# Decays of a selective scan in four buffers, the fourth in SBUF, each made one scan earlier

## What is computed

```
h  = layernorm(x) * (1 + scale) + shift;  h = h[:, idx]
xm, z = split(h @ W_in);  xm = silu(causal_conv(xm) + conv_b)
dtr, B, C = split(xm @ W_xp)                    # 64, 16, 16 wide
dt = softplus(dtr @ W_dt + b_dt)                # 1024 channels
for t:  hst = hst * exp(dt_t * A) + (dt_t * x_t) * B_t      # 1024 channels x 16 states
        y_t = sum_s hst * C_t
y = (y + xm * D) * silu(z);  out = x + gate * (y @ W_out)[:, idx]
```

## Time and profile before

| | before |
|---|---|
| median of 3 runs | 3013.91 us (3012.91 to 3016.35) |
| the profiled execution's own time | 3009.61 us |
| its span in the profile | 3007.8 us |
| DVE busy, share of the span | 2466.3 us, 82% |
| PE busy | 2648.0 us, 88% |
| POOL busy | 1883.4 us, 63% |
| ACT busy | 1621.8 us, 54% |
| TensorE clock granted, mean | 0.949 |

### The profile page before, as it was taken

How to read it: one execution, slowest core, us unless ns; L and a number is a source line. 1 busy time by engine, 2 the same in 40 slices (tenths; PEclk the granted TensorE clock), 3 DMA queues, 4 the chain that set the end, 5 groups by cost and what they waited for, 6 DMA issues and landing times. The chain is left out here.

```text
span 3007.8 us, 31819 instructions
## 1 busy us (share of the span) xinstructions
PE 2648.0 (88%) x10790; PEld 1499.2 (50%) x10790; DVE 2466.3 (82%) x3111; ACT 1621.8 (54%) x2444; POOL 1883.4 (63%) x822
## 2 busy tenths in 40 slices
PE   7999999999999877988988988988888897897974
PEld 3555555555555354554554554455455455454542
DVE  3566556666656599999999999999999998999993
ACT  1221322331332576776875875776676687586550
POOL 0131121222122396897998899799799799889991
PEclk9999999999999878999989999999999998998976
DMA  6102231231233444555664575665575566566653
GB/s 216 36 28 85 69 106 42 91 112 36 91 112 116 135 98 97 118 126 119 151 148 122 143 164 115 146 158 120 133 161 130 133 148 147 126 142 137 171 122 75
DMA packets 261604, 355.39 MB, mean 118 GB/s; under 512 B 21597, under 2 KB 115937, under 8 KB 261434
## 3 DMA queue, kind: packets, MB, share of 16 engines
q1 hardware_dynamic: 202024, 246.38, 26.8%
q0 software_dynamic: 55680, 105.93, 20.1%
q10 hardware_dynamic: 3730, 0.96, 0.2%
HBM read 215.56 MB, written 71.58 MB: 95 GB/s over the span
## 5 line engine op out<-in xcount | busy, mean ns | idle before, releaser
L2073 POOL TENSOR_TENSOR hs<-slots,b_wide 128x2048 f32<-128x2048 f32 x255 | 1270.5, 5011 | 142.8 <-PE bank L1589 142.6
L2267 DVE TENSOR_TENSOR_SCAN hs<-bank,hs 128x512 f32<-128x512 f32 x1024 | 1224.5, 1215 | 30.3 <-ACT bank L1846 25.3
L1846 ACT ACTIVATE bank<-dt,decay 128x512 f32<-128x512 f32 x1022 | 698.6, 691 | 540.7 <-DVE hs L2267 538.5
L1589 PE MATMUL bank<-ident,hs 128*128 128x128 f32 x4096 | 676.1, 295 | 240.1 <-DVE acc L2285 181.0
L1589 PEld LDWEIGHTS bank<-ident,hs 128*128 128x128 f32 x4096 | 515.1, 150 | 724.3 <-issue 264.0
L2285 DVE SCALAR_TENSOR_TENSOR acc<-bank,c_t,acc 128x512 f32<-128x512 f32 x772 | 566.4, 734 | 43.0 <-PE bank L1589 40.2
L1541 PE MATMUL bank<-h_t,w_in 128*128 128x512 f32 x1024 | 510.8, 608 | 1.4 <-ACT h_t L1764 1.2
L2121 POOL DMA_DIRECT2D acc<-scaled x252 | 291.2, 1155 | 49.2 <-DMA acc<-scaled 35.0
L982 POOL TENSOR_TENSOR y_rs<-y_var,mhalf 128x8 f32<-128x8 f32 x8 | 15.8, 1972 | 393.5 <-DVE y_var L355 393.5
L1641 PE MATMUL bank<-w_y,values 128*128 128x512 f32 x512 | 253.0, 600 | 1.3 <-DVE values L2389 1.3
L800 PE MATMUL bank<-z_t,w_k 128*128 128x512 f32 x512 | 223.0, 594 | 4.3 <-DVE k_t L1009 3.2
(11 more groups left out here) (180 smaller groups left out, 3344.3 us busy)
## 6 DMA issues: line engine op xcount, KB each, us to landing
b_wide<-b_rows SPq DMA_DIRECT2D x256, 256.0 KB, 3.6
acc<-scaled POOLq DMA_DIRECT2D x252, 256.0 KB, 5.3
w_in<-in_L_cond_W_in SPq DMA_DIRECT2D x128, 256.0 KB, 4.4
res<-in_x SPq DMA_DIRECT2D x8, 2048.0 KB, 10.0
h_tiles<-h_t SPq DMA_DIRECT2D x56, 256.0 KB, 2.8
h_in<-h_tiles SPq DMA_DIRECT2D x56, 256.0 KB, 4.1
x_rows<-w_part POOLq DMA_DIRECT2D x28, 512.0 KB, 6.8
x_rows<-res SPq DMA_DIRECT2D x6, 2048.0 KB, 7.3
```

The source lines that it names most:

```text
L1589: last = nc.tensor.transpose(bank[:, j * P:(j + 1) * P], hs[:, slot, j, t * P:(t + 1) * P], ident[:, :])
L1846: nc.scalar.activation(decay_banks[N % 3][:, :], dt[:, H % 2, j, :], ACT.Exp, scale=g.decay[:, 4 * (H % 2) + j, s:s + 1]).then_inc(da_read ...
L2073: nc.gpsimd.tensor_tensor(hs[:, U % RING, :, :], slots[:, H % SLOTS, :, :], b_wide[:, U % B_RING, :].unsqueeze(1).to_broadcast([P, 4, CHUNK]),
L2267: nc.vector.tensor_tensor_scan(block, decay_banks[N % 3][:, :], block, 0.0, ALU.mult, ALU.add).then_inc(scanned, 1)
```

## The change

Four edits. First, a fourth decay buffer, `decay_tile`, is added in SBUF, and the decays go round four buffers instead of three. ACT makes decay N+4 in the step in which it made decay N+3, behind the same scan. The scans with N % 4 == 3, the fourth of each unit, 256 in all, now read their decay from SBUF; their other input, `hs`, always lay there. Second, the sum of the step sizes' second half on POOL moves from unit 7 to unit 9. Third, the first projection of a batch waits for each modulated group just ahead of the matmul that reads it, not for the last three groups ahead of the first matmul. Fourth, a small tile of row statistics, `raw`, is laid over 24 columns of `cols` that layer 0 no longer needs, which makes room for the new buffer.

```diff
+DECAY_RING = 4
-ADD_DT_AT = (28, 7)
+ADD_DT_AT = (28, 9)
-        g.raw = sb("raw1", [P, CT, 6])
+        g.raw = g.cols[:, 0:6 * CT].rearrange("p (t s) -> p t s", t=CT)
...
-        state_banks, decay_banks, work_banks = banks[0:2], banks[3:6], [banks[6], banks[7], banks[2]]
+        decay_tile = sb("decay_tile", [P, CHUNK])
+        state_banks, decay_banks, work_banks = banks[0:2], [*banks[3:6], decay_tile], [banks[6], banks[7], banks[2]]
...
-                    if stage == "xm" and m == 0:
-                        for i in range(KD)[-place.ring:]:
-                            need(pe, *read_by(place, "h", i))
-                for k in ks:
+                for k in ks:
+                    if stage == "xm" and m == 0:
+                        need(pe, *read_by(place, "h", k))
                     last = nc.tensor.matmul(...)
...
-                need(act, scanned, N - 2)
-                nc.scalar.activation(decay_banks[N % 3][:, :], dt[:, H % 2, j, :], ACT.Exp,
+                need(act, scanned, N - (DECAY_RING - 1))
+                nc.scalar.activation(decay_banks[N % DECAY_RING][:, :], dt[:, H % 2, j, :], ACT.Exp,
...
-                    if N + 3 < BLOCKS * BATCH:
-                        decays(N + 3)
+                    if N + DECAY_RING < BLOCKS * BATCH:
+                        decays(N + DECAY_RING)
...
+                decays(3)
                 for b in range(BATCH):
                     turn(b)
...
-                nc.vector.tensor_tensor_scan(block, decay_banks[N % 3][:, :], block, 0.0, ALU.mult, ALU.add)
+                nc.vector.tensor_tensor_scan(block, decay_banks[N % DECAY_RING][:, :], block, 0.0, ALU.mult, ALU.add)
```

More of the change, by code:

```diff
@@ L2266, in scan @@
                 block = hs[:, N // 4 % RING, N % 4, :]
-                nc.vector.tensor_tensor_scan(block, decay_banks[N % 3][:, :], block, 0.0, ALU.mult, ALU.add).then_inc(scanned, 1)
+                nc.vector.tensor_tensor_scan(block, decay_banks[N % DECAY_RING][:, :], block, 0.0, ALU.mult, ALU.add).then_inc(scanned, 1)
             def scan_on(it, b, c, q):
```

## The result

The changed kernel takes 3391.7 us (3389.08 to 3397.18, 4 runs) against 3013.41 us of the kernel before in the same session. The ratio is 1.126, 95% interval 1.124 to 1.128: 378 us slower. The direction and the mechanism were those forecast. The size was not: the loss is more than twice the forecast one, and the time lies above the range.

A forecast was written before the change was run, and what follows sets the result against it. The prediction took DVE, busy 96% of the scans' stretch, to set the pace. 3009.6 + 203 - 20 - 9 - 3 = 3180.6, with 4.3 for the median of runs 3185 us; range 2998 to 3300.

The forecast's parts named there:

- Part 2: Fourth scans on DVE, reading both inputs from SBUF, block against POOL's reading instructions: 203 us of stalls, bounds 86 and 422.
- (a): Rival: a scan doesn't contend for SBUF as a product does, so only small gains remain: 3002 us, chance 0.17.
- (c): Rival: scans don't block, and each decay wait won returns as a PE wait: 3014 us, within 6; chance 0.05.
- (b): Rival: the block is real, but POOL's products fall in step behind the fourth scan: 3030 us, up to 3045; chance 0.08.
- The term of the stalls: Time fourth scans on DVE stand blocked by POOL: pairs 99 and 68 us, lone products 36, in sum 203 us.
- The 225 lone products: POOL products outside pairs: most fall just behind the fourth scan; two stalls per batch of 2.25 us, 36 us.
- the 30 pairs: On POOL, 15 step-size sums and 15 dt_x, each followed by a product without a DMA issue between: 99 and 68 us.
- The walk through units 26 to 28: A step-size sum and its product, traced with the new rule: fourth scans wait 0.54 and 4.0 us, together 4.5.
- The half of PE's waits taken back: While DVE stands, PE and ACT go on, so half of DVE's 40.2 us of waits for PE goes: -20 us.
- Part 1: Decays on ACT one scan ahead: nearly all 31 decay waits go, some return; gain 9 us, bounds 0 and 25.3.
- Part 3: Step-size sum on POOL at unit 9: scans wait less for late products; -3 us, bounds 0 and 5.0.
- Part 4: PE's waits by group and `raw` laid over `cols`: no gain and no cost, 0.

The follow-up runs named there:

- the banks: Changed kernel with the decays back in three PSUM banks, other edits kept: 3009.9 us, 0.9988 against the kernel before.
- the memset: Changed kernel with GpSimd's product of each unit replaced by a memset that reads nothing: 3033.7 us, one run.
- the drained kernel: Changed kernel in which GpSimd waits for its own semaphore after each product, step-size sum and dt_x: 3260.9 us, 1.084 against the kernel before.
- the kernel without the lead: Changed kernel with the fourth buffer in SBUF, but decays made as early as before: 3390.6 us, 1.124 against the kernel before.
- the memset pair: GpSimd's product replaced by a memset in the changed kernel and in the kernel before: 3033.7 and 2991.1 us, one run each.
- the second place: Changed kernel with the buffer order turned, so each unit's second scan reads its decay from SBUF: 3597.7 us, one run.

## Why the prediction was right and wrong

**Part 2, the mechanism: right.** The prediction took from plain products that a scan with two SBUF inputs is blocked while GpSimd reads. Fourth scans of up to 11.8 us beside others of 1.2, and a time that returns to before with the banks (3009.9), show it; the memset shows that it takes GpSimd's reads. By the Trainium skill ("SBUF — State Buffer", section "Who interferes with whom") the second comer is blocked until the first is finished; the runs agree: 64 of the 92 long scans ended 1.1 us after the first instruction's end, and products that came second waited for the scan. The other 28 were held for longer than one instruction, as below. Rivals (a) and (c), that a scan is exempt, fell, and so did (b), that products fall in step behind the scans.

**Part 2, the size: the step that failed.** The term of the stalls was 203 us and measured 412. Three things bear on it.

- "The 225 lone products: ... I take two stalls per batch of half a product, 2.25, 36 us." Sorted by what the scan met, the stalls with no sum or `dt_x` in them come to 275 us in 76 scans. This is 239 us above the term, more than the whole error of 209. In 63 of them, 152 us, the scan was held by one product, for 2.4 us on average: the price of one was right, and their number, two per batch or 16 in all, was a quarter of the true one. In the other 13, 122 us, it was held by two products in a row. Two assumptions went into the number. One was that products released by transposes begin behind the fourth scan. Where DVE has two taps between the third scan and the fourth, they begin ahead of it. The timeline of the changed kernel, DVE, then POOL, at unit 19 of the fourth batch:

```profile
2087.29 1.52 DVE L2219 SCALAR_TENSOR_TENSOR slots<-bank,taps,slots 128x510 f32<-128x510 f32 x2
2088.73 5.08 DVE L2269 TENSOR_TENSOR_SCAN hs<-decay_tile,hs 128x512 f32<-128x512 f32 x1
...
2088.24 4.49 POOL L2075 TENSOR_TENSOR hs<-slots,b_wide 128x2048 f32<-128x2048 f32 x1 [0.76 <-PE bank L1590]
```

  The product was released while the taps ran, 0.5 us before its scan was due. There are 13 such scans, with 52 us; in all, 29 scans, with 66 us, met a product ahead of which GpSimd had idled. The larger part, 47 scans with 208 us, met a product that GpSimd came to late, straight from other work. The prediction named this kind ("Only those that POOL starts late, behind its DMA issues, straddle") and undercounted it. The second assumption, that the order is right again after a stall, holds for the next unit in 67 of the 92 cases and fails in 25. What makes GpSimd late so often wasn't taken apart.
- "back-to-back POOL work is one block" was right but used too narrowly. The prediction counted only the 30 pairs as such. The walk through units 26 to 28 let the scan in at a product's end, ahead of the sum, though in the earlier trace rows the sum starts at 1958.17, before the product's end at 1958.26. In the trace after, the scan isn't let in there (2142.58 above). Chains of this kind held 28 scans for 259 us, some 165 of it past the end of the first instruction (157 in the expectation of the drained kernel). Drained, no chain is left and the kernel is 131 us faster. Product, DMA issue and product can be one block too, where the issue leaves no gap.
- The 30 pairs themselves were priced at 99 + 68 = 167 us and came to 137, differently spread: 15 of them held a scan, for 9 us on average, and the others cost next to nothing.

**The half of PE's waits taken back, 20 us: too high.** They went from 40.2 to 39.3. The kernel without the lead has 31.7, so the stalls seem to take back some 8 us, and the lead adds about as much again.

**Part 1, 9 us from the lead: too high.** Waits for decays fell by 25.3 us, all of them, but the kernel without the lead has the same time: there only 9.1 us of them are left, and with the lead most of these return as waits for PE. Without most stalls, with the memset, the lead is worth about 1 us. The reason given, that a decay wait won ahead of a sum returns in front of it, is what the memset pair shows, and it holds for more of them than the prediction allowed.

**Part 3, 3 us from unit 9: right**, 4.3 us measured alone, interval 1 to 7; no first tap waited for the sum in the changed kernel. **Part 4, nothing: right** within the 0.1% that the run of the waits by group can tell.

**The range.** Its upper end, 3300, lay below the random bound of the text, 422 us, which would have given 3014 + 422 less 30. That the stalls came out near it is chance. The bound takes 66% of the scans as blocked for 2.5 us each; measured are 36% (92 of 256) for 4.5 us. The same kind of scan lost 630 us at the second place and 165 us with products kept behind the fourth scan, so neither the walks nor the random figure stood in for the phase.

## What to carry over

Before a tile moves from PSUM to SBUF, count the SBUF inputs of every VectorE instruction that reads it, and look at what GpSimd does meanwhile: a second one costs nothing alone and here cost 1.6 us on average for each of 256 instructions. A block of this kind shows as a long maximum in one form of a line while VectorE looks busier, so compare forms, not the engine's share. If the phase isn't pinned by a wait, no single price holds: scans of this kind lost between 165 and 630 us here, around the 422 of a random phase. Give a range as wide as that, count all reading GpSimd work without a gap as one block, and count the products that start late in the timeline.

## What the runs showed of the hardware that was not expected

- Reading GpSimd instructions that follow each other with at most 0.09 us between them hold a waiting VectorE scan out (33 times of 34 in the changed kernel): 11.80 us over product, sum and product, with a DMA issue laid over the first two. With a DMA issue and at least 0.34 us between them the scan got in 26 times of 27. With a wait of GpSimd for its own semaphore it got in even with 0.08 us between, and the scan at the first place took 1.92 us.
- The block is mutual: products begun inside a fourth scan ended 4.31 to 4.35 us after it, 54 of 54.
- A GpSimd memset of 128x2048 (1.81 us) begun inside a scan with two SBUF inputs (1.21 us) delays neither; 115 scans overlapped one, the longest took 1.22 us.
- The TensorE clock granted in the stretch, as a share of 2.4 GHz, fell from 0.93 to 0.87, a mixture of its two levels, with PE busy 1634 of 1920 us before and 1721 of 2301 after; PE busy time in the stretch rose by 87 us for the same matmuls. No run here separates that from the stalls, in which PE stands idle.
